# The row quantisation of an FP4 feed-forward stage, split over four tiles and made two groups ahead

## The chip, the cores and the metric

The kernel runs on one core of a Trainium2 chip. The core has five engines that run side by side and wait for one another by semaphores: TensorE (PE), VectorE (DVE), ScalarE (ACT), GpSimd (POOL) and SyncE (SP), which only starts transfers. The metric is the device time of one execution in microseconds (us). Lower is better.

## The reference

`x` has 4 x 1024 rows of 256 numbers. Six steps follow one another, each with a layer norm of its own in front: an FP4 feed-forward, a local attention, the same FP4 feed-forward again, a mixture of experts, a causal attention, and the mixture of experts again. Only the FP4 feed-forward is touched:

```python
def fp4_quant_dequant(x):              # blocks of 16 along the last dim
    scale = jnp.maximum(jnp.max(jnp.abs(xb), axis=-1, keepdims=True) / 6.0, 1e-12)
    xn = xb / scale
    idx = jnp.searchsorted(_MID, jnp.abs(xn))
    return (_GRID[idx] * jnp.sign(xn) * scale).reshape(shape)
fp4_linear = lambda x, w: einsum('bsk,nk->bsn', fp4_quant_dequant(x), fp4_quant_dequant(w))
h = silu(fp4_linear(x, w_gate)) * fp4_linear(x, w_up)      # 256 -> 704
x = x + 0.5 * fp4_linear(h, w_down)                        # 704 -> 256
```

Both the normalised rows and `h` are quantised, so every tile passes through the quantisation twice.

## The kernel before

All of `x` stays on chip in `X`: 32 tiles of 128 rows. Four tiles are a group, so a stage has 8 groups. `fp4_ffn` is one FP4 stage; each engine runs a function `step` once a tile. The first 24 tiles are three turns of a hardware loop over eight tiles (two groups), the last eight are written out. In `step(n, g, s, end)` `n` is the tile, `g` its group, `j = s % 4` its place in the group.

*The rows* of a group are made by the helpers of the class `Fp4Rows`, each for 4 x 256 numbers per partition at once, in this order:

1. `stats` (VectorE): mean and variance (L129, L132, L134, L237).
2. `rstd` (GpSimd): the power of -1/2 and the shift (L139, L244).
3. `normalise` (ScalarE): four activations from `X` into `xn` (L250).
4. `scales` (VectorE): the largest number of each block of 16, the scale and its inverse (L177, L179, L181, L185).
5. `divide` (GpSimd): `xn` times the inverse (L190).
6. `rounding` (VectorE): the magic number of each element (L204, L207), added (L209) and subtracted again (L216).
7. `rescale` (GpSimd): times the scale (L190).
8. TensorE transposes `xn` (L594) and ScalarE copies it into `xT` (L651), which has two buffers.

Before, all that is in one buffer `xn`. So the rows of group g + 2 can be begun only when those of g + 1 have been transposed, at j = 1 of group g. The order is written out by hand: VectorE does stats at j = 2 and scales at j = 3 for group g + 2, and the whole rounding for g + 1 at j = 0; GpSimd does rstd at j = 2, divide at j = 3 and rescale at j = 0; ScalarE normalises at j = 2.

*A tile* in step n: TensorE transposes h of tile n (L625), then multiplies gate and up of tile n + 2 (L605), then down of tile n (L639). ScalarE copies the transposed h (L674 to L676), applies silu to tile n + 2 (L659) and at j = 1 copies the transposed rows. VectorE does its part of the rows first; then in `make_h` the product of silu and up (L523), the scales of h (L177, L179, L181), the division (L195) and the rounding up (L204, L207, L209) for tile n + 2; then it adds the down product of tile n to `X` (L557). GpSimd does its part of the rows and then finishes h in `h_finish` (L567, L190).

The waits that tie them: the gate matmuls of tile n + 2 wait until the L523 of tile n + 1 has read the bank of the up product (`h_ok`); L523 waits for the up matmuls and silu; the down matmuls wait until L557 of the tile before has read their bank; `h_finish` waits for the L209 of its tile. VectorE and the other engines work strictly in the written order.

Before the loop there is a prologue: rows of group 1 and h of tiles 0 and 1. The rows of group 0 are made in the stage before.

Of the kernel before, what the change touches and what calls it, by code (L numbers as in the profile page):

```python
# [27 lines left out]
GT = 4  # L28
# [167 lines left out]
                                          op0=ALU.mult, op1=ALU.mult)  # L196


def fp4_round_up(nc, a, magic):

    nc.vector.tensor_scalar(magic.bitcast(U32), a.bitcast(U32), EXP_BITS, HALF_BIT,  # L204
                            ALU.bitwise_and, ALU.bitwise_or)
    nc.vector.drain()
    nc.vector.tensor_scalar(magic, magic, 1.5, RND, ALU.max, ALU.mult)  # L207
    nc.vector.drain()
    return nc.vector.tensor_tensor(a, a, magic, ALU.add)  # L209


# [7 lines left out]
class Fp4Rows:  # L219


    def __init__(self, ch, name, ctx):
        self.ch = ch
        self.xn = ch.sb(name + "xn", [P, GT, D], ctx=ctx)
        self.magic = ch.sb(name + "xmagic", [P, GT * D], ctx=ctx)
        self.xs = ch.sb(name + "xs", [P, 3, XB], ctx=ctx)
        self.nmean = ch.sb(name + "nmean", [P, GT], ctx=ctx)
        self.shift = ch.sb(name + "shift", [P, GT], ctx=ctx)
        self.flat = self.xn[:, :, :].rearrange("p t d -> p (t d)")
        (self.stats_ok, self.rstd_ok, self.xn_ok, self.scaled, self.divided, self.rounded, self.quantised) = (  # L230
            ch.sem("fp4_" + k) for k in ("stats", "rstd", "xn", "x_scaled", "x_div", "x_round", "x_quant"))

# [10 lines left out]
        nc.gpsimd.drain()  # L243
        nc.gpsimd.tensor_tensor(self.shift[:, :], self.nmean[:, :], ch.rstd[:, :], ALU.mult).then_inc(self.rstd_ok, 1)  # L244

    def normalise(self, act, g):
        ch = self.ch
        act.wait_ge(self.rstd_ok, g + 1)
        for j in range(GT):
            last = ch.nc.scalar.activation(self.xn[:, j, :], ch.tile(g * GT + j), ACT.Identity,  # L250
                                           bias=self.shift[:, j:j + 1], scale=ch.rstd[:, j:j + 1])
        last.then_inc(self.xn_ok, 1)

    def scales(self, dve, g):
        dve.wait_ge(self.xn_ok, g + 1)
        fp4_scale(self.ch.nc, self.flat, XB, self.xs[:, 0, :], self.xs[:, 1, :], self.xs[:, 2, :]
                  ).then_inc(self.scaled, 1)

    def divide(self, pool, g):
        pool.wait_ge(self.scaled, g + 1)  # L260
        fp4_times(self.ch.nc.gpsimd, self.flat, XB, self.xs[:, 2, :]).then_inc(self.divided, 1)

    def rounding(self, dve, g):
        dve.wait_ge(self.divided, g + 1)
        fp4_round(self.ch.nc, self.flat, self.magic[:, :]).then_inc(self.rounded, 1)

    def rescale(self, pool, g):
        pool.wait_ge(self.rounded, g + 1)
        fp4_times(self.ch.nc.gpsimd, self.flat, XB, self.xs[:, 1, :]).then_inc(self.quantised, 1)


def prepare(ch, x, w_gate, w_up, w_down, a, rows):

    nc = ch.nc
    with ExitStack() as ctx:
# [90 lines left out]
        @block.vector  # L366
        def _(dve):
            def scale_down(m):
                raw, n = mats[m]
                fp4_scale(nc, raw[:, 0:n], n // BLK, amax, sc[:, m, :], rinv)  # L370
                nc.vector.drain()
                fp4_times(nc.vector, raw[:, 0:n], n // BLK, rinv)
                nc.vector.drain()

            def round_up_again(m):
                raw, n = mats[m]
                fp4_round(nc, raw[:, 0:n], magic[:, 0:n])
                nc.vector.drain()
                fp4_times(nc.vector, raw[:, 0:n], n // BLK, sc[:, m, :]).then_inc(quant, 1)

            for raw in (gate, up):
                nc.vector.memset(raw[chunk_rows(FC - 1):P, (FC - 1) * D:FC * D], 0.0)
            nc.vector.drain()
            dve.wait_ge(loaded_w[0], 16 * 2)
            scale_down(0)
            round_up_again(0)
            dve.wait_ge(loaded_g0, 16)
            rows.stats(dve, 0)
            dve.wait_ge(loaded_w[1], 16 * 2)
            scale_down(1)  # L390
            round_up_again(1)
            rows.scales(dve, 0)
            dve.wait_ge(loaded_w[2], 16)
            scale_down(2)
            rows.rounding(dve, 0)
            round_up_again(2)

        @block.tensor
# [76 lines left out]
def fp4_ffn(ch, name, first, rows):  # L475
# [10 lines left out]
    with ExitStack() as ctx:  # L486
# [30 lines left out]
        @block.vector  # L517
        def _(dve):
            def make_h(n, buf, first_two=False):

                dve.wait_ge(up_ok, n + 1)
                dve.wait_ge(silu_ok, n + 1)
                nc.vector.tensor_tensor(h[:, buf, :].rearrange("p (b n) -> p b n", b=2),  # L523
                                        sg[:, :].rearrange("p (b n) -> p b n", b=2),
                                        ps[:, UP:UP + 2, 0:FH], ALU.mult).then_inc(h_ok, 1)
                nc.vector.drain()
                s = hs[:, buf, :, :]
                fp4_scale(nc, h[:, buf, :], HB, s[:, 0, :], s[:, 1, :], s[:, 2, :], tie=False)
                nc.vector.drain()
                if not first_two:  # L530
                    dve.wait_ge(h_quant, n - 1)
                fp4_divide(nc, h[:, buf, :], HB, s[:, 2, :])
                nc.vector.drain()
                fp4_round_up(nc, h[:, buf, :], hmagic[:, buf % 2, :]).then_inc(h_round, 1)

            dve.sem_inc(h_turned, 1)
            if first:
                dve.wait_ge(ch.loaded_x, 16 * BATCHES)
            rows.stats(dve, 1)
            make_h(0, 0, True)  # L540
            rows.scales(dve, 1)
            make_h(1, 1, True)

            def step(n, g, s, end):
                j = s % GT
                if j == 0 and has(g, 1):
                    rows.rounding(dve, g + 1)
                if j == 2 and has(g, 2):
                    rows.stats(dve, g + 2)
                if j == 3 and has(g, 2):  # L550
                    rows.scales(dve, g + 2)
                if exists(n, 2):
                    make_h(n + 2, (s + 2) % 4)
                if not first and isinstance(n, int) and n == TILES - 2:
                    next_stats(ch, dve, ch.sem("moe_stats"))
                dve.wait_ge(down_ok, n + 1)
                nc.vector.scalar_tensor_tensor(out=ch.tile(n), in0=ps[:, DOWN, 0:D], scalar=0.5,  # L557
                                               in1=ch.tile(n), op0=ALU.mult, op1=ALU.add
                                               ).then_inc(x_added, 1)
            turns(dve, step)  # L560

        @block.gpsimd
        def _(pool):
# [6 lines left out]

            rows.rstd(pool, 1)
            h_finish(0, 0)
            rows.divide(pool, 1)
            h_finish(1, 1)

            def step(n, g, s, end):
                j = s % GT
                if j == 0 and has(g, 1):
                    rows.rescale(pool, g + 1)
                if j == 2 and has(g, 2):  # L580
                    rows.rstd(pool, g + 2)
                if j == 3 and has(g, 2):
                    rows.divide(pool, g + 2)
                if exists(n, 2):
                    h_finish(n + 2, (s + 2) % 4)
            turns(pool, step)
# [2 lines left out]

        @block.tensor  # L590
        def _(pe):
            def x_turn(g, c):
                for j in range(GT):
                    last = nc.tensor.transpose(ps[:, XTURN, j * P:(j + 1) * P],  # L594
                                               xn[:, j, c * P:(c + 1) * P], ch.ident[:, :])
                last.then_inc(x_turned, 1)

            def gate_up(n, g, s):
# [21 lines left out]
            def step(n, g, s, end):  # L620
# [10 lines left out]
                    gate_up(n + 2, g + (1 if j >= GT - 2 else 0), s + 2)  # L631
                if j == 1 and not end:
                    pe.wait_ge(rows.quantised, g + 2)
                    x_turn(g + 1, 0)
                pe.wait_ge(h_stored, n + 1)
                pe.wait_ge(x_added, n + 1)
                for r in range(FC):
# [3 lines left out]
                last.then_inc(down_ok, 1)  # L641
                if j == 1 and not end:
                    pe.wait_ge(x_stored, 2 * g + 3)
                    x_turn(g + 1, 1)
            turns(pe, step)

        @block.scalar
        def _(act):
# [1 line left out]
                act.wait_ge(x_turned, 2 * g + c + 1)  # L650
                nc.scalar.activation(xT[:, par, c, :], ps[:, XTURN, :], ACT.Copy).then_inc(x_stored, 1)  # L651

            def x_normalise(g):
                act.wait_ge(x_turned, 2 * g)
                rows.normalise(act, g)

            def silu(n):
                act.wait_ge(gate_ok, n + 1)
# [5 lines left out]
            x_store(0, 0, 0)  # L664
            x_store(0, 1, 0)
            silu(0)
            x_normalise(1)
            act.wait_ge(h_ok, 1)
            silu(1)

            def step(n, g, s, end):
# [6 lines left out]
                if exists(n, 2):  # L678
                    act.wait_ge(h_ok, n + 2)
                    silu(n + 2)  # L680
                if j == 1 and not end:
                    x_store(g + 1, 0, par)
                    x_store(g + 1, 1, par)
                if j == 2 and has(g, 2):
                    x_normalise(g + 2)
            turns(act, step)


def local_attention(ch, name, next_rows):
# [7 lines left out]
    with ExitStack() as ctx:  # L697
# [18 lines left out]
        with nc.Block() as block:  # L716
# [4 lines left out]
            def _(dve):  # L721
# [48 lines left out]
                for k in range(GROUPS + 4):  # L770
# [12 lines left out]
                    if k == 8:  # L783
                        next_rows.scales(dve, 0)
                    if k == 9:
                        next_rows.rounding(dve, 0)

            @block.gpsimd
            def _(pool):
# [1542 lines left out]
```

## Time and profile before

| | us |
|---|---|
| median of 3 runs | 2328.38 |
| lowest and highest | 2323.71, 2336.24 |
| profiled execution | 2326.32 |
| its span | 2324.6 |
| TensorE matmuls busy | 1960.7 (84%) |
| VectorE busy | 1764.5 (76%) |
| ScalarE busy | 958.9 (41%) |
| GpSimd busy | 907.5 (39%) |

The span goes from the first instruction to the last; the profiled execution's own time is 1.7 us longer. Times in rows are microseconds from the start of the span. `L605` is line 605 of the kernel; a line can be that of a helper that several stages use, and then the names of the tiles tell which work it is: `f_xn` and `f_xs` are rows, `f_h` and `f_hs` are h. A busy engine is not always the one that sets the end, so the order of time and the waits are read beside the shares. The granted clock is what the chip let TensorE run at: 1.0 is 2.4 GHz, 0.5 is 1.2 GHz.

### The profile page before, as it was taken

How to read it: one execution, taken by the hardware profiler on the slowest of the kernel's cores; microseconds unless marked ns; L12 is line 12 of the kernel's file. 1: busy time of each engine (PE TensorE's matmuls, PEld its weight loads, DVE VectorE, ACT ScalarE, POOL GpSimd, SP SyncE). 2: the span in 40 equal slices, each digit the busy share in tenths (PEclk: the TensorE clock that was granted, in tenths of full speed). 3: DMA queues.
4: the chain of work that ended last, by engine and by line, in shares of the span. 5: the costliest groups of instructions: out<-in, count | busy, mean ns of one | idle time of the engine just before them, and what ended most of it. 6: DMA issues, size and time to landing. Idle time of an engine off the chain costs nothing. (4 is left out here: it accounts for less than half of the span.)

```text
span 2324.6 us, 36254 instructions
## 1 busy us (share of the span) xinstructions
PE 1960.7 (84%) x11363; PEld 1301.0 (56%) x11363; DVE 1764.5 (76%) x3598; ACT 958.9 (41%) x1892; POOL 907.5 (39%) x910
## 2 busy tenths in 40 slices
PE   2899997889999747989978599999999995398998
PEld 1566665756666426877866233333333363287787
DVE  7798874578887667877978577777777646687788
ACT  1222223322222443433557255555555537143345
POOL 2444442134444467887245300000000026588853
PEclk9999997989999858999989699999999996599999
DMA  5000000100000342223526534334334006222246
GB/s 177 1 0 0 0 0 14 42 0 1 0 0 0 97 159 64 92 87 101 170 69 168 98 55 70 51 54 69 50 55 70 2 1 195 75 89 89 89 148 191
DMA packets 116655, 156.59 MB, mean 67 GB/s; under 512 B 20966, under 2 KB 85772, under 8 KB 115980
## 3 DMA queue, kind: packets, MB, share of 16 engines
q1 hardware_dynamic: 99840, 112.83, 20.9%
q0 software_dynamic: 14400, 40.41, 5.6%
q8 instruction: 89, 1.46, 0.3%
q10 hardware_dynamic: 2252, 1.29, 0.2%
q14 instruction: 74, 0.61, 0.1%
HBM read 107.00 MB, written 47.20 MB: 66 GB/s over the span
## 5 line engine op out<-in xcount | busy, mean ns | idle before, releaser
L2021 DVE TENSOR_REDUCE t_nm<-ps 128x1 f32<-128x512 f32 (+3 forms) x768 | 390.9, 553 | 106.3 <-PE ps L2111 53.5
L2087 ACT ACTIVATE t_E<-ps 128x1024 f32<-128x1024 f32 (+3 forms) x384 | 295.0, 808 | 248.0 <-PE ps L2139 194.9
L1507 PE MATMUL ps<-m_w,m_xT 128*128 (+1 forms) x1248 | 347.1, 414 | 0.8 <-DVE m_xT L1587 0.8
L1507 PEld LDWEIGHTS ps<-m_w,m_xT 128*128 128x128 f32 x1248 | 222.5, 191 | 38.2 <-issue 1.4
L567 POOL TENSOR_TENSOR f_h<-f_h,f_hmagic 128x704 f32<-128x704 f32 x64 | 108.1, 1689 | 293.4 <-DVE f_h L209 293.4
L605 PE MATMUL ps<-wgT,f_xT 128*128 128x352 f32 x512 | 187.8, 516 | 38.5 <-DVE f_h L523 36.4
L2006 POOL COPY t_Va<-t_V 128x128 f32<-128x128 f32 x64 | 16.1, 295 | 491.7 <-DVE t_mp L2032 491.5
L2136 PE MATMUL ps<-t_Qs,t_Ks 98*128 98x512 bf16 (+3 forms) x768 | 199.8, 341 | 6.0 <-DMA t_Qs<-t_mT 4.1
L1525 PE MATMUL ps<-m_w,m_hT 128*128 (+1 forms) x1248 | 199.7, 296 | 0.5 <-DVE m_hT L1604 0.5
L639 PE MATMUL ps<-wdT,f_hT 128*128 128x256 f32 (+1 forms) x768 | 189.5, 389 | 7.4 <-DVE X L557 5.4
L1559 ACT ACTIVATE m_hT<-ps 128x256 fp32r<-128x256 f32 x208 | 80.1, 385 | 227.9 <-PE ps L1516 226.7
L1594 DVE TENSOR_TENSOR m_ab<-ps,m_b 128x512 f32<-128x512 f32 x208 | 143.1, 688 | 37.4 <-PE ps L1507 35.4
L639 PEld LDWEIGHTS ps<-wdT,f_hT 128*128 128x128 f32 (+1 forms) x768 | 139.2, 189 | 52.8 <-issue 27.1
L2153 PE MATMUL ps<-t_E,t_Va 128*32 128x512 f32 (+3 forms) x1536 | 166.2, 505 | 0.0
L2106 PE MATMUL ps<-t_Ks,t_Qs 48*128 48x512 bf16 (+3 forms) x384 | 135.1, 352 | 35.6 <-DVE t_nm L2021 26.5
L605 PE MATMUL ps<-wuT,f_xT 128*128 128x352 f32 x512 | 164.1, 464 | 0.0
L1525 PEld LDWEIGHTS ps<-m_w,m_hT 128*128 128x128 f32 x1248 | 161.8, 190 | 0.9 <-DVE m_hT L1604 0.9
L1423 POOL DMA_INDIRECT m_picked_out<-m_y,m_dst_row x144 | 144.4, 1003 | 41.4 <-issue 32.9
L1413 POOL DMA_INDIRECT m_xg<-m_rows,m_src_row x144 | 140.3, 974 | 49.8 <-issue 36.1
L605 PEld LDWEIGHTS ps<-wgT,f_xT 128*128 128x128 f32 x512 | 103.3, 212 | 97.4 <-issue 54.6
L2106 PEld LDWEIGHTS ps<-t_Ks,t_Qs 48*128 48x128 bf16 x384 | 35.9, 93 | 204.0 <-DVE t_nm L2021 190.5
L2108 PE MATMUL ps<-t_Ko,t_Qo 48*128 48x512 bf16 (+3 forms) x384 | 135.1, 352 | 0.0
(296 smaller groups left out, 3950.0 us busy)
## 6 DMA issues: line engine op xcount, KB each, us to landing
m_raw<-in_L_ffn_rw SPq DMA_DIRECT2D x48, 256.0 KB, 3.3
t_parts<-t_qkv_part SPq DMA_DIRECT2D x64, 192.0 KB, 2.8
t_Qs<-t_parts SPq DMA_DIRECT2D x96, 128.0 KB, 4.0
t_Ks<-t_parts SPq DMA_DIRECT2D x96, 128.0 KB, 6.6
m_yl<-m_picked_out SPq DMA_DIRECT2D x40, 256.0 KB, 3.2
m_rows<-m_xn SPq DMA_DIRECT2D x16, 512.0 KB, 4.3
m_xg<-m_rows SPq DMA_DIRECT2D x64, 128.0 KB, 2.8
m_y<-m_picked_out SPq DMA_DIRECT2D x24, 256.0 KB, 3.3
```

The lines of the kernel that those rows point to most:

```text
L605: last = nc.tensor.matmul(ps[:, bank + half, 0:FH], xT[:, par, c, j * P:(j + 1) * P], w[:, c, half * FH:(half + 1) * FH], start=c == 0, st ...
L639: last = nc.tensor.matmul(ps[:, DOWN, 0:D], hT[0:rr, r, :], ch.wdT[0:rr, r, :], start=r == 0, stop=r == FC - 1)
L1413: nc.gpsimd.indirect_dma_start(out=xg[:, i % RING, :], out_offset=None, in_=rows[:, :], in_offset=bass.IndirectOffsetOnAxis(ap=src_row[:, ...
L1423: nc.gpsimd.indirect_dma_start(out=picked_out[:, :], out_offset=bass.IndirectOffsetOnAxis(ap=dst_row[:, i:i + 1], axis=0), in_=y[:, i % RI ...
L1507: last = nc.tensor.matmul(ps[:, H1 + u, :], xT[:, u, kx, k, :], of_expert(w1, kw, e, k), start=n == 0, stop=n == 3 * DC - 1)
L1525: last = nc.tensor.matmul(ps[:, OUT + u, 0:D], hT[:, u, kh, f, :], of_expert(w2, kw, e, f), start=n == 0, stop=n == 3 * FK - 1)
L1594: tt(ab[:, u, :], ps[:, H1 + u, :], row_of(b1, e), ALU.add).then_inc(ab_ok, 1)
L2021: nc.vector.tensor_reduce(dst, ps[:, bank, 0:n], AX_X, ALU.max, negate=True).then_inc(emptied, 1)
L2087: nc.scalar.activation(E[:, s % NPB, :, 0:n], ps[:, bank:bank + 2, 0:n], ACT.Exp, scale=float(HD) ** -0.5).then_inc(e_ok, 1)
L2106: mine = [nc.tensor.matmul(ps[:, banks[0], 0:n], Qs[c][0:LEAD, 2 * pair, rows], Ks[c][0:LEAD, 2 * pair, cols], start=True, stop=not diag), ...
L2136: last = nc.tensor.matmul(o[:, 0:n], Ks[c][:, h, kb * P:(kb + 1) * P], Qs[c][:, h, q0:q0 + n], start=True, stop=not diag)
L2153: last = nc.tensor.matmul(ps[h * WIN:(h + 1) * WIN, YB, off:512], Va[:, c, kb, h * VW:h * VW + WIN], E[:, (2 * k + h // 2) % NPB, h % 2, 0 ...
```

## The change

`xn` gets two buffers, one for each parity of the group. With them the rows of group g + 2 no longer wait for the transposes of g + 1, and all parts are for group g + 2, one part a tile:

| j | VectorE before | VectorE after | GpSimd before | GpSimd after | ScalarE before | ScalarE after |
|---|---|---|---|---|---|---|
| 0 | rounding (g+1) | stats | rescale (g+1) | rstd | | normalise |
| 1 | | scales | | divide | | |
| 2 | stats | magics | rstd | | normalise | |
| 3 | scales | rounding: add, subtract | divide | rescale | | |

The old `rounding` is cut in two: `magics` (L204, L207) and the new `rounding` (L209, L216). The prologue now makes the rows of group 1 complete, rounding and rescale too. The other uses of the class, in front of the stages, call both halves one behind the other. The diff, cut to its core:

```diff
-        self.xn = ch.sb(name + "xn", [P, GT, D], ctx=ctx)
+        self.xn = ch.sb(name + "xn", [P, 2, GT, D], ctx=ctx)
...
-    def rounding(self, dve, g):
+    def magics(self, dve, g, par=0):
         dve.wait_ge(self.divided, g + 1)
-        fp4_round(self.ch.nc, self.flat, self.magic[:, :]).then_inc(self.rounded, 1)
+        fp4_magic(self.ch.nc, self.flat[par], self.magic[:, :])
+
+    def rounding(self, par=0):
+        nc, flat = self.ch.nc, self.flat[par]
+        nc.vector.tensor_tensor(flat, flat, self.magic[:, :], ALU.add)
+        nc.vector.drain()
+        nc.vector.tensor_tensor(flat, flat, self.magic[:, :], ALU.subtract).then_inc(self.rounded, 1)
...
             rows.stats(dve, 1)
             make_h(0, 0, True)
-            rows.scales(dve, 1)
+            rows.scales(dve, 1, 1)
             make_h(1, 1, True)
+            rows.magics(dve, 1, 1)
+            rows.rounding(1)
 
             def step(n, g, s, end):
                 j = s % GT
-                if j == 0 and has(g, 1):
-                    rows.rounding(dve, g + 1)
+                par = (s // GT) % 2
+                if j == 0 and has(g, 2):
+                    rows.stats(dve, g + 2)
+                if j == 1 and has(g, 2):
+                    rows.scales(dve, g + 2, par)
                 if j == 2 and has(g, 2):
-                    rows.stats(dve, g + 2)
+                    rows.magics(dve, g + 2, par)
                 if j == 3 and has(g, 2):
-                    rows.scales(dve, g + 2)
+                    rows.rounding(par)
...
             h_finish(0, 0)
-            rows.divide(pool, 1)
+            rows.divide(pool, 1, 1)
             h_finish(1, 1)
+            rows.rescale(pool, 1, 1)
 
             def step(n, g, s, end):
                 j = s % GT
-                if j == 0 and has(g, 1):
-                    rows.rescale(pool, g + 1)
-                if j == 2 and has(g, 2):
+                par = (s // GT) % 2
+                if j == 0 and has(g, 2):
                     rows.rstd(pool, g + 2)
+                if j == 1 and has(g, 2):
+                    rows.divide(pool, g + 2, par)
                 if j == 3 and has(g, 2):
-                    rows.divide(pool, g + 2)
+                    rows.rescale(pool, g + 2, par)
...
                 if exists(n, 2):
                     act.wait_ge(h_ok, n + 2)
                     silu(n + 2)
+                if j == 0 and has(g, 2):
+                    act.wait_ge(x_turned, 2 * g + 2)
+                    x_normalise(g + 2, 1 - par)
                 if j == 1 and not end:
                     x_store(g + 1, 0, par)
                     x_store(g + 1, 1, par)
-                if j == 2 and has(g, 2):
-                    x_normalise(g + 2)
```

`has(g, 2)` is true for groups 0 to 5; the last two groups have no parts.

## Rows read from the trace of the kernel before

**Rows 1.** Busy us by stage (the two FP4 stages): PE, PEld, DVE, ACT, POOL, clock, DMA.
```profile
57.66:373.00 315.34, 288.54 (x1144) 196.06 (x1145) 261.85 (x413) 78.33 (x173) 135.83 (x92) 0.97 0.00 0
...
463.77:787.70 323.93, 293.18 (x1152) 198.77 (x1151) 265.50 (x435) 80.63 (x177) 136.91 (x94) 0.95 0.00 1
```

**Rows 2.** Waits of VectorE and of TensorE, 100 to 340 us: total, times, longest.
```profile
DVE f_h L523 <- PE ps L605: 11.1, 6, 3.5
...
PE ps L605 <- DVE f_h L523: 15.4, 6, 2.8
```

**Rows 3.** Order of time on VectorE, one group: start, us, engine, line, operation.
```profile
164.25 0.88 DVE L523 TENSOR_TENSOR f_h<-f_silu,ps 128x704 f32<-128x704 f32 x1
...
170.34 0.88 DVE L523 TENSOR_TENSOR f_h<-f_silu,ps 128x704 f32<-128x704 f32 x1
...
172.28 1.16 DVE L179 TENSOR_SCALAR f_hs<-f_hs 128x44 f32<-128x44 f32 x1
...
177.39 1.40 DVE L129 BATCH_NORM_STATS2 st<-X 128x6 f32 x4
...
180.45 0.88 DVE L523 TENSOR_TENSOR f_h<-f_silu,ps 128x704 f32<-128x704 f32 x1
...
186.46 1.21 DVE L177 TENSOR_REDUCE f_xs<-f_xn 128x64 f32<-128x1024 f32 x1
...
189.47 0.88 DVE L523 TENSOR_TENSOR f_h<-f_silu,ps 128x704 f32<-128x704 f32 x1
...
195.50 2.05 DVE L204 TENSOR_SCALAR f_xmagic<-f_xn 128x1024 uint32<-128x1024 uint32 x1
...
199.41 1.23 DVE L209 TENSOR_TENSOR f_xn<-f_xn,f_xmagic 128x1024 f32<-128x1024 f32 x1
...
201.86 0.88 DVE L523 TENSOR_TENSOR f_h<-f_silu,ps 128x704 f32<-128x704 f32 x1
```

**Rows 4.** Order of time on TensorE: four gate products of one group.
```profile
165.28 2.61 PE L605 MATMUL ps<-wgT,f_xT 128*128 128x352 f32 x8 [2.68 <-DVE f_h L523]
...
174.87 2.63 PE L605 MATMUL ps<-wgT,f_xT 128*128 128x352 f32 x8
...
183.30 2.53 PE L605 MATMUL ps<-wgT,f_xT 128*128 128x352 f32 x8
...
191.62 2.53 PE L605 MATMUL ps<-wgT,f_xT 128*128 128x352 f32 x8
```

**Rows 5.** Order of time on GpSimd and VectorE, where both work on rows and h.
```profile
83.65 2.00 DVE L207 TENSOR_SCALAR f_xmagic<-f_xmagic 128x1024 f32<-128x1024 f32 x1
...
85.24 1.66 POOL L190 TENSOR_TENSOR f_h<-f_h,f_hs 128x704 f32<-128x704 f32 x1
85.73 2.25 DVE L209 TENSOR_TENSOR f_xn<-f_xn,f_xmagic 128x1024 f32<-128x1024 f32 x1
...
88.05 1.23 DVE L216 TENSOR_TENSOR f_xn<-f_xn,f_xmagic 128x1024 f32<-128x1024 f32 x1
...
186.28 1.69 POOL L567 TENSOR_TENSOR f_h<-f_h,f_hmagic 128x704 f32<-128x704 f32 x1 [4.32 <-DVE f_h L209]
...
195.33 1.67 POOL L567 TENSOR_TENSOR f_h<-f_h,f_hmagic 128x704 f32<-128x704 f32 x1 [3.77 <-DVE f_h L209]
```

**Rows 6.** Instructions on the tile f_xn: ns least/median/most.
```profile
L209 DVE TENSOR_TENSOR f_xn<-f_xn,f_xmagic x16: 1224/1226/2249, 41.8 to 724.8; 128x1024 f32<-128x1024 f32 x16
```

**Rows 7.** Order of time on ScalarE: the normalise of one group.
```profile
182.10 2.08 ACT L250 ACTIVATE f_xn<-X,f_shift,rstd 128x256 f32 x4 [3.79 <-POOL f_shift L244]
```

**Rows 8.** Order of time at the start and near the end of both FP4 stages.
```profile
89.19 0.88 DVE L523 TENSOR_TENSOR f_h<-f_silu,ps 128x704 f32<-128x704 f32 x1
...
318.64 5.03 PE L605 MATMUL ps<-wgT,f_xT 128*128 128x352 f32 x8 [2.69 <-DVE f_h L523]
...
331.08 2.61 PE L605 MATMUL ps<-wgT,f_xT 128*128 128x352 f32 x8
...
495.00 0.88 DVE L523 TENSOR_TENSOR f_h<-f_silu,ps 128x704 f32<-128x704 f32 x1
...
728.30 5.03 PE L605 MATMUL ps<-wgT,f_xT 128*128 128x352 f32 x8 [2.67 <-DVE f_h L523]
```

More of the change, by code:

```diff
@@ L196, in fp4_divide, with fp4_magic @@
                                           op0=ALU.mult, op1=ALU.mult)
-def fp4_round_up(nc, a, magic):
+def fp4_magic(nc, a, magic):
     nc.vector.tensor_scalar(magic.bitcast(U32), a.bitcast(U32), EXP_BITS, HALF_BIT,
@@ L208, in fp4_round_up @@
     nc.vector.drain()
+def fp4_round_up(nc, a, magic):
+    fp4_magic(nc, a, magic)
     return nc.vector.tensor_tensor(a, a, magic, ALU.add)
@@ L228, in __init__ @@
         self.shift = ch.sb(name + "shift", [P, GT], ctx=ctx)
-        self.flat = self.xn[:, :, :].rearrange("p t d -> p (t d)")
+        self.flat = [self.xn[:, k, :, :].rearrange("p t d -> p (t d)") for k in range(2)]
         (self.stats_ok, self.rstd_ok, self.xn_ok, self.scaled, self.divided, self.rounded, self.quantised) = (
@@ L244, in rstd, with normalise @@
         nc.gpsimd.tensor_tensor(self.shift[:, :], self.nmean[:, :], ch.rstd[:, :], ALU.mult).then_inc(self.rstd_ok, 1)
-    def normalise(self, act, g):
+    def normalise(self, act, g, par=0):
         ch = self.ch
@@ L249, in normalise, with scales, divide, rescale @@
         for j in range(GT):
-            last = ch.nc.scalar.activation(self.xn[:, j, :], ch.tile(g * GT + j), ACT.Identity,
+            last = ch.nc.scalar.activation(self.xn[:, par, j, :], ch.tile(g * GT + j), ACT.Identity,
                                            bias=self.shift[:, j:j + 1], scale=ch.rstd[:, j:j + 1])
         last.then_inc(self.xn_ok, 1)
-    def scales(self, dve, g):
+    def scales(self, dve, g, par=0):
         dve.wait_ge(self.xn_ok, g + 1)
-        fp4_scale(self.ch.nc, self.flat, XB, self.xs[:, 0, :], self.xs[:, 1, :], self.xs[:, 2, :]
+        fp4_scale(self.ch.nc, self.flat[par], XB, self.xs[:, 0, :], self.xs[:, 1, :], self.xs[:, 2, :]
                   ).then_inc(self.scaled, 1)
-    def divide(self, pool, g):
+    def divide(self, pool, g, par=0):
         pool.wait_ge(self.scaled, g + 1)
-        fp4_times(self.ch.nc.gpsimd, self.flat, XB, self.xs[:, 2, :]).then_inc(self.divided, 1)
-    def rounding(self, dve, g):
+        fp4_times(self.ch.nc.gpsimd, self.flat[par], XB, self.xs[:, 2, :]).then_inc(self.divided, 1)
+    def magics(self, dve, g, par=0):
         dve.wait_ge(self.divided, g + 1)
-        fp4_round(self.ch.nc, self.flat, self.magic[:, :]).then_inc(self.rounded, 1)
-    def rescale(self, pool, g):
+        fp4_magic(self.ch.nc, self.flat[par], self.magic[:, :])
[4 more added lines that the diff above has]
+        nc.vector.tensor_tensor(flat, flat, self.magic[:, :], ALU.subtract).then_inc(self.rounded, 1)
+    def rescale(self, pool, g, par=0):
         pool.wait_ge(self.rounded, g + 1)
-        fp4_times(self.ch.nc.gpsimd, self.flat, XB, self.xs[:, 1, :]).then_inc(self.quantised, 1)
+        fp4_times(self.ch.nc.gpsimd, self.flat[par], XB, self.xs[:, 1, :]).then_inc(self.quantised, 1)
 def prepare(ch, x, w_gate, w_up, w_down, a, rows):
@@ L394, in _ @@
             scale_down(2)
-            rows.rounding(dve, 0)
+            rows.magics(dve, 0)
+            rows.rounding()
             round_up_again(2)
@@ L591, in _, with x_turn @@
         def _(pe):
-            def x_turn(g, c):
+            def x_turn(par, c):
                 for j in range(GT):
                     last = nc.tensor.transpose(ps[:, XTURN, j * P:(j + 1) * P],
-                                               xn[:, j, c * P:(c + 1) * P], ch.ident[:, :])
+                                               xn[:, par, j, c * P:(c + 1) * P], ch.ident[:, :])
                 last.then_inc(x_turned, 1)
@@ L633, in step @@
                     pe.wait_ge(rows.quantised, g + 2)
-                    x_turn(g + 1, 0)
+                    x_turn((s // GT + 1) % 2, 0)
                 pe.wait_ge(h_stored, n + 1)
@@ L643, in step @@
                     pe.wait_ge(x_stored, 2 * g + 3)
-                    x_turn(g + 1, 1)
+                    x_turn((s // GT + 1) % 2, 1)
             turns(pe, step)
@@ L651, in x_store, with x_normalise @@
                 nc.scalar.activation(xT[:, par, c, :], ps[:, XTURN, :], ACT.Copy).then_inc(x_stored, 1)
-            def x_normalise(g):
-                act.wait_ge(x_turned, 2 * g)
-                rows.normalise(act, g)
+            def x_normalise(g, par):
+                rows.normalise(act, g, par)
             def silu(n):
@@ L666, in _ @@
             silu(0)
-            x_normalise(1)
+            x_normalise(1, 1)
             act.wait_ge(h_ok, 1)
@@ L785, in _ @@
                     if k == 9:
-                        next_rows.rounding(dve, 0)
+                        next_rows.magics(dve, 0)
+                        next_rows.rounding()
             @block.gpsimd
```

## The prediction

> **What bounds the kernel now.** I first cut the span into stages by busy time. The two FP4 stages take 315.3 and 323.9 us of 2324.6, and in both TensorE and VectorE are busy at once: 288.5 and 261.9 us, 293.2 and 265.5 us [rows 1]. Busy time doesn't say which sets the pace, since VectorE's gaps between dependent operations don't count as busy. The waits do. In the steady part of the first stage TensorE waits 15.4 us for the product L523 (six times, once a group), while all that VectorE waits for is 11.1 us [rows 2].
>
> The order of time shows why. VectorE goes through a group of four tiles without a break: the L523 of step j = 0 starts at 164.25 and the same one a group later at 201.86, 37.61 us [rows 3]. Its own part of each tile, from L523 to the end of the X addition L557, is 6.02 us (180.45 to 186.46, 189.47 to 195.50). The rest is the next group's rows: stats 3.06 (177.39 to 180.45), scales 3.01 (186.46 to 189.47), and at j = 0 the whole rounding 6.36 (195.50 to 201.86): magic numbers 3.91 (to 199.41), then two additions 2.45. The step with no part takes 7.05 (170.34 to 177.39), because its small L179, on 44 numbers a row, waits for GpSimd (1.16 us). Sum: 4 x 6.02 + 3.06 + 3.01 + 6.36 + about 1.0 = 37.5.
>
> TensorE needs less. An ordinary step, gate to gate, is 8.32 (183.30 to 191.62), the step with the x transposes 9.59 (165.28 to 174.87) [rows 4]; 3 x 8.32 + 9.59 = 34.55. The missing 2.7 to 3.0 us is the one stall in front of the gate after the rounding (2.68). So VectorE is the bound and that stall is its image: to spread VectorE's parts over four tiles splits the stall, and brings time only where VectorE itself gets shorter or where TensorE was late.
>
> **What the change does to VectorE's group.** No instruction is added or removed in the steady loop. What changes is which GpSimd work each one meets. GpSimd starts finishing a tile's h 0.17 us before VectorE starts the next step's part (195.33 against 195.50): L567, 1.69 us where nothing holds it, then L190, to some 3.1 us behind the part's start [rows 5].
> - j = 0, stats: meets the same h finish as before: 3.06.
> - j = 1, scales: 3.01 as before; GpSimd's divide comes behind it as before.
> - j = 2, magics alone: the same pair beside the same h finish, 3.91.
> - j = 3, the two additions: before, they ran when GpSimd had finished, 2.45. Now they start with the h finish.
> - the step without a part is gone, so its 1.0 us is gone.
>
> What do two additions beside the h finish cost? This group of rows never has them there, but the first one has: the addition L209 that began at 85.73, while L190 ran from 85.24 for 1.66 us (to 86.90), took 2.25 us, ending 1.08 us after it [rows 5]. Of the 16 additions L209 on rows (median 1.226) two took that long [rows 6], the first in each stage's loop. L207 in front of it (83.65, 2.00) was held in the same manner. So I lay the step out, 0 being the start of the part: L567 runs from -0.17 to 1.52; L209 is held till then and ends at 2.60; GpSimd's L190 is held meanwhile and takes the 1.25 us that are left of it after 85.65, to 3.85; L216 is held till then, and ends at 4.93; the next L523 starts at 4.84 (L216 to L523 is 1.14, from 88.05 to 89.19). The part costs 4.84 and not 2.45. If both additions got in before L190, the part would be 3.7, but the h finish and the rescale behind it would then run until 7.0 and hold L179 by 1.4: 5.1, the same within 0.3. Bounds: 2.45 + 0.7 (nothing held but L179, which then meets the rescale) = 3.15; and, with GpSimd first both times, 5.3 + 1.0 = 6.3. I take 4.84, from the row that shows this very instruction held.
>
> Here the skill weighs in. The Trainium skill (SBUF — State Buffer, Who interferes with whom) says that a VectorE instruction with two SBUF inputs and a GpSimd instruction that reads SBUF exclude one another, the later one fully. The trace agrees: L209 with both inputs in SBUF was held (2.25), L523 with one input in PSUM never was (0.88). By the rule every addition at j = 3 is held; without it the two long rows would be chance and the first rival would come out.
>
> New group: 4 x 6.02 + 3.06 + 3.01 + 3.91 + 4.84 = 38.9 against 37.5: **VectorE loses 1.4 us a group**, over the six groups that have parts.
>
> **TensorE beside it.** A gate can't start before the last L523 has ended, 1.03 us after that starts (164.25, 165.28). With L523 at 0, 9.0, 19.0 and 29.9, and 38.9 for the next group, the gates of j = 1, 2, 3, 0 start at 1.0, 10.6, 20.0 and 30.9; the up matmuls end some 5.06 later, always 2.4 to 3.3 us before VectorE asks for them. TensorE idles 4.4 us a group: 1.1, 2.6 and 0.8. The rows' other work stays hidden: ScalarE's normalise (four activations, 2.08 us [rows 7]) starts 1.65 us after L523 of j = 0, ends at 3.7, the scales want it at 6.0; the h copies of the next tile queue behind it and are done at 4.9, while TensorE's down matmuls want them at 6.5. GpSimd's divide is done (3 us after the scales) before the magics, and the rescale a whole step before TensorE's transposes. No DMA is moved.
>
> **What TensorE's clock did.** After eight of the 14 long stalls ahead of a gate in both stages the granted clock was at its lower level, 1.2 and not 2.4 GHz, and the eight gate matmuls took 4 to 5 us in place of 2.5; the third of the eight is at 318.64, the last at 728.30 [rows 8]. The first of these steps took 12.44 (to 331.08), 2.85 more than 9.59. Before, VectorE waited for such gates, as the step behind had no part. Now there is a gap of 3.0 us there, which hides them. Only the last one in each stage, where VectorE has no parts any more, shows.
>
> **The ends.** The change makes group 2's rows during group 0, so the first group has one rounding more than before and the last but one has one less. At the start: rounding as before, then stats, some 2.3 us with a short wait for the rescale; L523 of the first step comes at 91.5 and 497.3, where it was 89.19 and 495.00 [rows 8]. From there to the gate of j = 1 in the last group but one: 6 x 38.94 - 3.06 (no stats) - 6.03 (back to the last L523) + 1.03 + 8.32 + 0.25 (a down matmul that waits for L557) = 234.15. That gives 325.6 and 731.4, against 318.64 and 728.30: **+7.0 and +3.2**. The step there was a slow one in both, 2.85 too long; if none is, **-5.7**. Sum +4.5. The chance of a slow one in the new tails I take as before, 8 in 14 for each of two, 2.85 each: +3.3. Together +7.8 on the profiled execution's 2326.32: **2334**. That execution was 2.1 below the median of the three runs (2328.38); how often the clock falls differs between runs, and I leave that in the range. The rest of the program (local attention, expert and attention stages, some 1680 us) is only shifted. 0.5%, 11.6 us, is about what a measurement of this kernel can tell from no change; +5.6 against the median is inside.
>
> **Rivals.**
> 1. *The additions are not held* (3.15). For it: 14 of 16 L209 took 1.23. Against: none of these had GpSimd beside it. The group would be 37.2, the longest stall 1.5 and so perhaps no fall of the clock at all; the same sum gives 314.6 and 720.4, that is -4.0, -7.9 and -5.7: -17.6, 2309. Faster. 18%.
> 2. *VectorE's bound does not move*: held additions, but one of them slips into a gap, so that the group stays at 37.5 to 38. Then 12 x 1.2 us go from the forecast: 2320 to 2326. 15%.
> 3. *Slower by over 0.5%*: the clock. TensorE idles 4.4 us a group, not 2.7, at three gates. If it were granted 1.2 GHz behind the 2.6 us stall in every group and stayed there through the up matmuls too, the loss would be twice 2.4 (5.03 against 2.61 for eight matmuls), 1.8 past the gap of 3.0, in each of 12 groups: +22 on the forecast, 2356. It decides from 3.0 us a group on. For it: more idle time. Against: no slow step in the trace lost over 2.9 us, and the longest stall is no longer than before. 14%.
> 4. The forecast, +4.5 with 0 to 2 slow steps and one or two tenths a group either way: 2328 to 2341. 53%.
>
> The range 2315 to 2346 leaves out most of rival 1 and the far end of 3. Faster by over 0.5% (under 2316.7): 0.18; slower (over 2340): 0.19, all of rival 3 and the top of 4; same 0.63.
>
> **What would show it.** In order of time on VectorE: L216 and L209 of the rows at 1.9 to 2.5 us each, where they were 1.23; L207 at 1.7 as before; L179 of h never over 0.3; L523 of j = 0 each 38.9 us; no VectorE waits for L605 between the start and the last two groups (11.1 before in the first). On TensorE: waits for L523 twice or three times a group, together 4.4 us, slow gates hidden. Rows at 1.23 and a group at 37.2 mean rival 1. VectorE waiting for the up matmuls behind slow gates means rival 3. A change in the stages after the FP4 ones would be something I have not seen.

## The result, and the profile after

| | before | after |
|---|---|---|
| median, us | 2327.11 (4 runs) | 2344.98 (4 runs) |
| lowest and highest | 2323.71, 2336.24 | 2340.49, 2348.49 |
| ratio to before, 95% | | 1.0082 (1.0056 to 1.0108) |
| the same, repeated (29 and 12 runs) | 2327.22 | 2343.60, 1.0069 (1.0043 to 1.0094) |

The change costs 16 to 19 us, 0.7 to 0.8%. I had said 2334, no measurable change. The time lies in the stated range of 2315 to 2346, but near its upper end, where I had put 0.19, and it is slower beyond doubt: both intervals lie above 1.

The page of the changed kernel, its span and busy times:

```profile
span 2338.7 us, 36234 instructions
...
PE 1971.5 (84%) x11363; PEld 1297.7 (55%) x11363; DVE 1781.3 (76%) x3598; ACT 958.0 (41%) x1892; POOL 921.2 (39%) x910
```

VectorE has as many instructions as before (3598) and is 16.8 us busier: instructions became longer. The two FP4 stages of both kernels, each from its first product of silu and up to its last X addition (us, then busy time of PE, PEld, DVE, ACT, POOL, and the clock), first before, then after:

```profile
68.17:375.30 307.13, 281.71 (x1128) 192.07 (x1128) 259.88 (x404) 73.48 (x166) 134.59 (x90) 0.97 0.00 0
473.99:784.90 310.91, 284.37 (x1128) 193.65 (x1128) 261.12 (x414) 73.71 (x166) 135.71 (x92) 0.96 0.00 0
```

```profile
68.61:384.80 316.19, 287.21 (x1128) 191.01 (x1128) 269.11 (x404) 72.67 (x166) 139.38 (x90) 0.97 0.00 0
480.86:800.42 319.56, 292.19 (x1128) 194.91 (x1128) 271.60 (x413) 72.53 (x165) 140.58 (x92) 0.95 0.00 0
```

The stages are 17.7 us longer together, with 19.7 us more busy time on VectorE for the same work. One group of the changed kernel in order of time on VectorE, which answers to [rows 3] (L530 is the old L523, L200 and L203 the magics, L269 and L271 the two additions):

```profile
160.92 0.88 DVE L530 TENSOR_TENSOR f_h<-f_silu,ps 128x704 f32<-128x704 f32 x1
...
166.94 1.40 DVE L129 BATCH_NORM_STATS2 st<-X 128x6 f32 x4
...
169.98 0.87 DVE L530 TENSOR_TENSOR f_h<-f_silu,ps 128x704 f32<-128x704 f32 x1
...
176.05 1.21 DVE L177 TENSOR_REDUCE f_xs<-f_xn 128x64 f32<-128x1024 f32 x1
...
179.06 0.87 DVE L530 TENSOR_TENSOR f_h<-f_silu,ps 128x704 f32<-128x704 f32 x1
...
185.16 2.05 DVE L200 TENSOR_SCALAR f_xmagic<-f_xn 128x1024 uint32<-128x1024 uint32 x1
...
187.28 1.72 DVE L203 TENSOR_SCALAR f_xmagic<-f_xmagic 128x1024 f32<-128x1024 f32 x1
...
189.22 0.89 DVE L530 TENSOR_TENSOR f_h<-f_silu,ps 128x704 f32<-128x704 f32 x1 [0.21 <-issue]
...
195.24 2.58 DVE L269 TENSOR_TENSOR f_xn<-f_xn,f_xmagic 128x1024 f32<-128x1024 f32 x1
...
197.89 2.25 DVE L271 TENSOR_TENSOR f_xn<-f_xn,f_xmagic 128x1024 f32<-128x1024 f32 x1
...
200.06 0.87 DVE L530 TENSOR_TENSOR f_h<-f_silu,ps 128x704 f32<-128x704 f32 x1
```

GpSimd in the last step of it, which answers to [rows 5]:

```profile
195.06 1.68 POOL L579 TENSOR_TENSOR f_h<-f_h,f_hmagic 128x704 f32<-128x704 f32 x1 [6.62 <-DVE f_h L209]
...
196.88 2.18 POOL L190 TENSOR_TENSOR f_h<-f_h,f_hs 128x704 f32<-128x704 f32 x1
```

The group is 39.14 us (160.92 to 200.06), the additions 2.58 and 2.25 where they were 1.23, and they alternate with GpSimd's two instructions: L579 ends at 196.74, the first addition at 197.82, L190 at 199.06, the second addition at 200.14. The waits in the first stage, 100 to 340 us, which answer to [rows 2]; first VectorE's, then TensorE's:

```profile
DVE f_h L530 <- PE ps L619: 3.8, 2, 2.2
```

```profile
PE ps L619 <- DVE f_h L530: 10.5, 11, 1.1
PE ps L639 <- POOL f_h L190: 3.8, 6, 0.6
PE ps L653 <- DVE X L569: 2.2, 9, 0.3
```

VectorE waits for no matmul until the parts end (the 3.8 us lie behind 318 us); TensorE waits more often and for less each time. At the end of a stage the trace shows something that I had not looked for. First the gate behind the last part and the two gates that follow it, then the last stall of each stage and the down matmuls of the last tile of the second stage, all on TensorE, after:

```profile
318.30 4.29 PE L619 MATMUL ps<-wgT,f_xT 128*128 128x352 f32 x8 [1.10 <-DVE f_h L530]
...
328.39 2.53 PE L619 MATMUL ps<-wgT,f_xT 128*128 128x352 f32 x8
...
337.88 2.60 PE L619 MATMUL ps<-wgT,f_xT 128*128 128x352 f32 x8
...
374.12 5.75 PE L653 MATMUL ps<-wdT,f_hT 128*128 128x256 f32 x12 [2.69 <-DVE X L569]
...
786.90 5.75 PE L653 MATMUL ps<-wdT,f_hT 128*128 128x256 f32 x12 [2.69 <-DVE X L569]
...
795.13 5.26 PE L653 MATMUL ps<-wdT,f_hT 128*128 128x256 f32 x12 [1.00 <-ACT f_hT L689]
```

and the same two stalls before:

```profile
367.32 3.02 PE L639 MATMUL ps<-wdT,f_hT 128*128 128x256 f32 x12 [2.70 <-DVE X L557]
...
776.94 3.02 PE L639 MATMUL ps<-wdT,f_hT 128*128 128x256 f32 x12 [2.69 <-DVE X L557]
```

The stall is the same, but the twelve down matmuls behind it ran at the clock's lower level in both stages of the changed kernel (granted clock 0.51 and 0.50) and in neither of the other (1.00).

### The profile page after: what moved, and what is told of

Its sections match the earlier page's. It is cut to its first block and busy times, and to the rows that moved or that the text cites. A ratio compares the mean times of both kernels' runs of the same rounds, so it can differ in the third digit from the quotient of the medians.

```text
span 2338.7 us, 36234 instructions
## 1 busy us (share of the span) xinstructions
PE 1971.5 (84%) x11363; PEld 1297.7 (55%) x11363; DVE 1781.3 (76%) x3598; ACT 958.0 (41%) x1892; POOL 921.2 (39%) x910
## 5 line engine op out<-in xcount | busy, mean ns | idle before, releaser
L579 POOL TENSOR_TENSOR f_h<-f_h,f_hmagic 128x704 f32<-128x704 f32 x64 | 108.1, 1689 | 319.5 <-DVE f_h L209 319.5
L653 PE MATMUL ps<-wdT,f_hT 128*128 128x256 f32 (+1 forms) x768 | 198.5, 402 | 11.9 <-DVE X L569 9.9
```

Of the source, the lines that this page charges most:

```text
L653: last = nc.tensor.matmul(ps[:, DOWN, 0:D], hT[0:rr, r, :], ch.wdT[0:rr, r, :], start=r == 0, stop=r == FC - 1)
```

## The experiments

A cut in a diff is marked by `...`. The kernel before was measured beside each set of runs, and its median differed: 2327.22 us beside runs 1 and 2, 2323.50 beside 3, 4 and 6, 2320.75 beside 7. So a ratio is to that median, and times of different sets are not compared. The times also carry noise from outside the FP4 stages: the part behind them takes 1538 to 1551 us in eight profiles of the two kernels, with no pattern. I read each run by its ratio and, from its profile, by VectorE's group (from L523 of j = 0 to the next) and by the end of a stage (from the last L523 to the last X addition). "Group" is the usual one in the loop; the first of a stage can be longer.

**1. Rounding in one piece (e1_whole).** Theory: GpSimd's h finish holds the two additions. Rivals: the ends of the stage, or the clock.

```diff
-                if j == 2 and has(g, 2):
-                    rows.magics(dve, g + 2, par)
                 if j == 3 and has(g, 2):
+                    rows.magics(dve, g + 2, par)
                     rows.rounding(par)
```

> The changed kernel with both halves of the row rounding at j = 3 (two buffers, two groups ahead and the prologue as changed). Theory of the held additions: magics and additions in one piece run past the h finish, as before the change; the additions take 1.23 us again, the part 6.4, the empty step at j = 2 gets its 1.0 back; group 37.5 instead of 39.1 us, twelve groups -19.6 us: 2325 (2320 to 2330), not slower than the kernel before. Rival, the ends (one group more at the start, the written order two groups ahead): group stays 39.1 or the loss sits outside the groups: 2340 or more. Rival, the clock (more and smaller TensorE idle): 2335 to 2345, with VectorE waiting for up matmuls.

Measured: 2322.17, 0.9972 of before (0.9948 to 0.9997). Group 37.5. The rows' rounding:

```profile
190.31 2.05 DVE L200 TENSOR_SCALAR f_xmagic<-f_xn 128x1024 uint32<-128x1024 uint32 x1
192.44 1.72 DVE L203 TENSOR_SCALAR f_xmagic<-f_xmagic 128x1024 f32<-128x1024 f32 x1
194.24 1.23 DVE L269 TENSOR_TENSOR f_xn<-f_xn,f_xmagic 128x1024 f32<-128x1024 f32 x1
195.54 1.22 DVE L271 TENSOR_TENSOR f_xn<-f_xn,f_xmagic 128x1024 f32<-128x1024 f32 x1
```

The additions are short again, and 21 us against the changed kernel's 2343.60 are gone. Two buffers and two groups ahead by themselves cost nothing; they may even gain.

**2. The additions a few instructions later (e2_adds_mid).**

```diff
-                if j == 3 and has(g, 2):
-                    rows.rounding(par)
+                mid = (lambda: rows.rounding(par)) if j == 3 and has(g, 2) else None
                 if exists(n, 2):
-                    make_h(n + 2, (s + 2) % 4)
+                    make_h(n + 2, (s + 2) % 4, mid=mid)
...
```

`make_h` runs `mid` behind the maximum of h (L177), and GpSimd's `rescale` goes behind its `h_finish`.

> The changed kernel with the two additions of the rows moved a few instructions later inside the same step (behind the maximum of h, L177, where GpSimd has nearly finished h), and GpSimd's rescale behind its h finish. Same instructions, same steps. Theory of the held additions: the first is held about 1 us (till 3.05 us behind the step's start), the second not at all; L269 about 2.1, L271 1.23; the step 9.5 in place of 10.85; group 37.8, twelve groups -17: 2328 (2323 to 2333). Rivals, the ends or the clock: no change from 2345, additions at 1.2 and the time lost elsewhere.

Measured: 2324.96, 0.9986 (0.9958 to 1.0015). Group 37.6 to 37.8.

```profile
194.00 2.16 DVE L271 TENSOR_TENSOR f_xn<-f_xn,f_xmagic 128x1024 f32<-128x1024 f32 x1
196.24 1.22 DVE L273 TENSOR_TENSOR f_xn<-f_xn,f_xmagic 128x1024 f32<-128x1024 f32 x1
```

One addition was held for about 1 us, the other was free, as laid out. The step has the same instructions; only the moment differs.

**3. Control: the rescale alone moved (e6_rescale_late).** In GpSimd's step, `rescale` behind `h_finish`, nothing else.

> Control for the run with the additions moved: the changed kernel with only GpSimd's rescale behind its h finish. Theory of held additions: they stay at 2.6 and 2.25, the group at 39.1 to 39.3; if the place of the rescale was what helped, the group is 37.8.

Measured: one run, 2345.12. Group 39.0 to 39.3, the additions as in the changed kernel, so the gain of run 2 comes from moving the additions:

```profile
195.72 2.58 DVE L269 TENSOR_TENSOR f_xn<-f_xn,f_xmagic 128x1024 f32<-128x1024 f32 x1
198.38 2.25 DVE L271 TENSOR_TENSOR f_xn<-f_xn,f_xmagic 128x1024 f32<-128x1024 f32 x1
```

**4. Magics moved too (e3_both_mid).**

```diff
+                mid = None
                 if j == 2 and has(g, 2):
-                    rows.magics(dve, g + 2, par)
+                    mid = lambda: rows.magics(dve, g + 2, par)
                 if j == 3 and has(g, 2):
-                    rows.rounding(par)
+                    mid = lambda: rows.rounding(par)
...
```

The rest is as in run 2.

> As the run with the additions behind the maximum of h, and the magics (j = 2) moved to the same place in their step. Theory of held instructions: L204 and L207 of the rows, 2.05 and 1.72 us beside the h finish, become about 1.6 and 0.6; the j = 2 step 8.3 in place of 9.9; VectorE's group 36.2, or 36.5 with a short wait for the up matmuls at j = 2; twelve groups -31 against the changed kernel: 2312 (2306 to 2318), 0.7% below the kernel before. If only the rounding's place mattered: 2325.

Measured: 2308.94, 0.9940 (0.9914 to 0.9965). Group 36.1 to 36.3. In its trace the magics and additions of the rows (L202, L205, L271, L273) are hardly held any more. The magics had been held all along, in the kernel before too: 2.05 and 1.72 us beside the h finish, 0.69 each here. VectorE now waits for TensorE's up matmuls twice a group:

```profile
180.63 0.89 DVE L532 TENSOR_TENSOR f_h<-f_silu,ps 128x704 f32<-128x704 f32 x1 [0.99 <-PE ps L622]
...
182.58 0.69 DVE L202 TENSOR_SCALAR f_xmagic<-f_xn 128x1024 uint32<-128x1024 uint32 x1
183.35 0.69 DVE L205 TENSOR_SCALAR f_xmagic<-f_xmagic 128x1024 f32<-128x1024 f32 x1
...
188.96 0.89 DVE L532 TENSOR_TENSOR f_h<-f_silu,ps 128x704 f32<-128x704 f32 x1 [0.68 <-PE ps L622]
...
190.90 1.41 DVE L271 TENSOR_TENSOR f_xn<-f_xn,f_xmagic 128x1024 f32<-128x1024 f32 x1
192.39 1.23 DVE L273 TENSOR_TENSOR f_xn<-f_xn,f_xmagic 128x1024 f32<-128x1024 f32 x1
```

This version beats both kernels. By the ratios (0.9940 and 1.0069) it saves some 30 us against the changed one, and its two stages took 602.7 us in its profile against 634.6, although both ended in the slow clock (19.8 us each).

**5. Repeats.** For the stage's end, three more profiles of each kernel.

> The changed kernel again, for a second profile and more times: 1.006 to 1.010 of the kernel before. VectorE's group 39.1 in every execution. If the slow clock at the end of both stages in the first profile is chance, it falls otherwise here, and the span changes with it by 2 to 8 us; if it belongs to the changed kernel, the down matmuls behind the last VectorE stall take 5.7 us again in both stages.

> The kernel before again, one look, for a second set of clock falls: VectorE's group 37.5 without falls; falls behind about half of the long stalls, each seen by VectorE as 1.5 to 2.8 us of waiting. The down matmuls behind the last stall of a stage: 3.0 if the fast ones were the rule, 5.7 in some if it is chance.

> The changed kernel, one more profile. Open: the stage's end (from the last product L530 to the last X addition), 14.2 us without a slow clock, was 16.9 and 19.8 us in the first profile and 15.8 and 19.8 in the second. If it belongs to the changed kernel, the second stage shows 19.8 again; if it is chance, 14.2 to 19.8. The groups 39.1 whatever the clock does, both stages together 628 to 636 us.

> The kernel before, one more profile: end of the second stage 14.2 us again if it belongs to the kernel, anything to 19.8 if chance. Both stages together 617 to 621 us, VectorE waiting 5 to 10 us a stage for up matmuls at the slow clock.

> As the other repeat of the changed kernel: second stage's end 19.8 if the kernel's own, 14.2 to 19.8 if chance; together 628 to 636.

> As the other repeat of the kernel before: second stage's end 14.2 if the kernel's own, else up to 19.8; together 617 to 621.

r1_after is the repeat in the table at the top. The ends of the first and the second stage, by profile: before 14.2 and 14.2, 15.8 and 14.2, 15.9 and 14.2, 15.8 and 15.9; after 16.9 and 19.8, 15.8 and 19.8, 16.9 and 19.9, 19.8 and 16.9. The runs on the way show the same scatter: 14.2 twice in run 1, 14.2 and 16.9 in run 2, 15.6 twice in run 3. My "19.8 in the second stage if it is the kernel's own" fell in the last profile, and "14.2 to 19.8 by chance" fits badly too: all eight ends of the changed kernel are slow. That the groups of the changed kernel would not mind the clock was right: 39.0 to 39.5 in all eight stages. The other five repeats are single runs, 2337.74, 2341.15 and 2321.60 us before, 2348.79 and 2339.87 after. These times overlap, as the part behind the stages differs by up to 11 us; the two FP4 stages together do not: 620.4, 621.8 and 612.5 before, 634.5 and 634.6 after. The latter fell in the expected 628 to 636, the former outside the expected 617 to 621 in both profiles that had it, because the falls of the clock inside the loop differ.

**6. Taking the last stall away (e4_after_end, e5_both_end).**

```diff
+                early = isinstance(n, int) and n == TILES - 3
...
+                    make_h(n + 2, (s + 2) % 4, mid=x_add if early else None)
...
```

`x_add` is the X addition of tile n.

> The changed kernel with one instruction moved, once a stage: the X addition of the last tile but two goes into the middle of the make_h of that step, ahead of the rest of it, so that the last stall of TensorE in a stage (2.69 us in front of the down matmuls) goes. It asks what the end of the stage cost the changed kernel: in both of its profiles the clock fell behind that stall in both stages (down matmuls 4.7 to 5.7 us, 3.0 without). Theory that this is 7 us of the loss: stall and falls go, -5.4 and -8: 2330. If the falls are tied to something else or come anyway: -5, 2338.

> Magics and additions behind the maximum of h, and the early X addition at the stage's end: the sum of both: group 36.5, the stage's end 2.7 us shorter, no fall there: 2304 (2298 to 2312), 1.0% below the kernel before.

Measured: 2349.90, 1.0111 (1.0078 to 1.0145), and 2310.46, 0.9943 (0.9924 to 0.9961). The first expectation failed. The second time lies in its range, but it is no faster than run 4 (0.9940), and the fall that I had expected to go came all the same (ends of 17.9 and 16.8 us). In the first of these kernels the trace shows that the stall only moved to the next wait, for h of the last tile from GpSimd, which the earlier addition had pushed back, and that the clock fell behind that one:

```profile
377.07 1.23 PE L645 MATMUL ps<-ident,f_h 128*128 128x128 f32 x6 [2.66 <-POOL f_h L192]
379.30 5.45 PE L659 MATMUL ps<-wdT,f_hT 128*128 128x256 f32 x12 [1.00 <-ACT f_hT L695]
```

Its stages took 316.0 and 315.5 us, no worse than those of the changed kernel; the part behind the stages took 1559 in that profile. Whether its slower median has another cause is open.

**7. Shifting the last stall (e7_shift8, e9_shift8b, e8_shift16, e10_both_shift8).**

```diff
+                if isinstance(n, int) and n == TILES - 4:
+                    for e in range(8):                       # 16 in e8_shift16
+                        nc.tensor.transpose(ps[:, XTURN, (e % 4) * P:(e % 4 + 1) * P], ...)
...
```

> The changed kernel with 8 useless transposes (some 1 us of TensorE work, results used by nothing) in the last group of each FP4 stage. If the moment of the last stall decides: in the second stage the down matmuls behind it take 3.0 and not 5.7 us and the end is 14.2 instead of 19.8 or 16.9, although work was added; 2338 (2333 to 2343). If the slow clock there belongs to the change: 1 us more a stage, 2346.

> The first of these once more: 3.0 us in the second stage again if the moment decides.

> The same with 16 transposes, some 1.9 us later: if the moment decides, the slow clock is back, shorter: down matmuls 4.7 us, end 15.8 to 16.9. If it is the amount of TensorE work in front: 3.0 as with 8.

> Magics and additions behind the maximum of h, with 8 useless transposes in the last group: without them both stages ended in 19.8 us; if the moment decides, 14.2, net 4.6 us a stage less in spite of the added work: 2300 (2295 to 2307), 1% below the kernel before. If not: 2311.

Measured, in the order of the expectations: 2337.33, 1.0078 (1.0051 to 1.0105); one run of 2350.04; one run of 2343.98; and 2308.68, 0.9925 (0.9890 to 0.9960). The first time is close to the 2338 that I had expected, but only because the kernel before was at 2320.75 here: by its ratio nothing was gained. The down matmuls behind the last stall of the second stage, with 8, with 16, and with 8 in the best kernel:

```profile
787.98 4.41 PE L657 MATMUL ps<-wdT,f_hT 128*128 128x256 f32 x12 [2.70 <-DVE X L569]
```

```profile
788.10 4.66 PE L657 MATMUL ps<-wdT,f_hT 128*128 128x256 f32 x12 [2.70 <-DVE X L569]
```

```profile
757.33 5.76 PE L660 MATMUL ps<-wdT,f_hT 128*128 128x256 f32 x12 [2.70 <-DVE X L572]
```

With the shift these matmuls took 4.4 to 4.7 us in the changed kernel, where without it they took 5.73 to 5.76 in seven of eight stages and 4.66 in one. They never took the 3.0 that I had expected with 8 transposes, and in the best kernel nothing changed. The ends with 8 were 18.5 us in three stages, where the last tile's down matmuls were slow too, and 15.8 in one; with 16 they were 15.9 and 15.8, in the best kernel 19.8 twice. The 4.7 us and the end of the 16 came out as expected, but the 3.0 with 8 that this rested on did not. One kernel ends differently from one execution to the next (16.9 or 19.8 in the same stage), so something beside its instructions decides. That it is the moment of the stall is my guess; with one or two profiles of each shift it is not shown.

## Why the prediction was wrong

From the first product of a stage to its last X addition, both stages together, us. "Before" is the execution that the prediction rests on; "after" is the mean of four:

| part | before | predicted | after |
|---|---|---|---|
| start, to the first product of the loop | 42.0 | 46.6 | 46.4 |
| loop and last two groups, to the last product | 547.6 | 550.8 | 551.8 |
| end, to the last X addition | 28.35 | 28.35 | 36.4 |
| sum | 617.9 | 625.7 | 634.6 |

- **The bound.** Right: VectorE sets the group's pace in both kernels, and splitting TensorE's stall brought nothing by itself (0.9972 in run 1, with one wait for L530 of up to 2.0 us a group, and 0.9986 in run 2, with no wait for it over 0.5). I had laid out TensorE's waits as 4.4 us a group, in pieces of 1.1, 2.6 and 0.8 ahead of three gates. The group shown has 0.9 and 1.1 ahead of two gates, 0.6 for h from GpSimd, whose L190 is held, and 0.25 twice for the X addition. In the waits of the first stage, those for L530 come to 1.8 us a group, with none over 1.1.
- **The held additions.** Right, in mechanism and size: L269 was laid out to end 2.60 us behind the start of the part and took 2.58; L271 2.26, took 2.25; the part 4.84, took 4.82. Rival 1 is dead; runs 1 to 3 show that the price hangs on when the additions run.
- **The group.** 38.94 predicted, 39.16 measured on average: +0.22 in ten groups, 2.2 us. It is mostly the magics' step (4.06 in place of 3.91, with 0.21 us of issue in front of the product) and the first group of the second stage (39.54).
- **Cover from falls of the clock.** Right: VectorE waited for no up matmuls inside the loop in any of eight stages; before, it did for some 10 us in six of eight, for 4.8 in one and for none in one.
- **The step ahead of the loop.** +2.3 a stage predicted, +2.15 measured.
- **The tails.** I allowed 3.3 us for slow gates where the parts end. Five of eight stages had one, and it cost 1.7 us each (a last group of 37.7 in place of 36.0), 2.1 a profile. With the groups that makes the +1.0 of the middle row.
- **The step that failed: "Only the last one in each stage ... shows".** I took the way from the last gates to the end of the stage as the same in both kernels, since it has the same instructions and stalls, and priced no fall there; I had looked at stalls ahead of gates only, not at the one ahead of the down matmuls. It measured 8.1 us more than the execution I built on, which had no slow end at all; the other three executions of the kernel before had, so against the mean of all four (30.0) it is 6.4. The forecast of both stages was 8.9 us short: 8.1 at the ends, 1.0 in the middle, -0.2 at the start. Between the means of four profiles each the stages grew by 16.4 us, where I had added 7.8; the runs' times say 16 to 19.
- **Rivals and sums.** Rival 3 had the right direction and the wrong place: the clock cost time at the ends, and nothing inside the loop. That the measured time still lies in the range is owed to the width that rival 3 gave it, not to the sum. Two sums of the rivals are slightly off: rival 1's group of 37.2 gives 315.2 and 721.0, not 314.6 and 720.4, and rival 2's groups give 2317 to 2323, not 2320 to 2326.
- **What stays open.** Why all eight ends of the changed kernel are slow and four of eight before. The change doesn't touch these instructions. It sets when they come, and the profile of a kernel with the same tail can show none (e1_whole: 14.2 and 14.2) or both (e3_both_mid). A shift did not do what I thought. So the 6.4 of 16.4 us at the ends could be luck in part, and so could some of the middle row: before, it was 547.6, 548.4, 549.7 and 538.8 us in the four profiles, by how often the clock fell, and 551.4 to 552.7 after. That VectorE is 19.7 us busier is not luck: each held addition took the same 2.58 or 2.25 us in all four profiles.

## What to carry to other kernels

When an order is spread out to shorten a stall, write down for each moved VectorE instruction what GpSimd does at that moment: two additions that meet GpSimd's work cost 2.4 us a group here, and splitting the stall brought nothing. Moved by two instructions (behind one that reads PSUM and one that only reduces) they are nearly free. Put the work that wasn't held here beside GpSimd's, and the rest behind it: that turned +0.7% into -0.6% with the same instructions. And when one profile is the base of a sum, ask of every stall in it, the last one too, whether the clock happened to hold there.

## What the runs showed of the hardware

- An addition on VectorE with both inputs in SBUF waits for a GpSimd instruction in progress that reads SBUF, and holds the next one: 1.23 us alone, 2.16 to 2.58 beside it, and GpSimd's L190 1.39 alone, 2.18 beside it. In the twelve profiles of both kernels and of runs 1 to 4, every held addition of the rows ended 1.08 us behind the end of the GpSimd instruction that held it. The Trainium skill (SBUF — State Buffer, Who interferes with whom) says that two such instructions contend and that the later one blocks fully, and the traces agree.
- The magics, with one input in SBUF, are held too: 2.05 and 1.72 us beside GpSimd's h finish, 0.69 each without it (run 4). The product of silu and up, with one input in PSUM, took 0.87 to 0.89 us everywhere, also beside GpSimd's L190 (179.06, where L190 ran from 179.22).
- The same twelve down matmuls behind the same stall of 2.69 us took 3.02, 4.4, 4.7 or 5.75 us in different executions and stages: the same idle time is followed by the lower clock (1.2 GHz) or not. The kernel before showed 3.02 in four of eight cases, the changed one never. I had not expected a price of up to 5.6 us a stage from one such stall. In the ends of 19.8 us the twelve down matmuls of the last tile were slow as well (5.26 us, where they take 3.05 at the full clock). A stall of 1.1 us can be followed by the lower clock too: the gate at 318.30 took 4.29 us at a granted clock of 0.60.
